# A second conditioning weight loaded in two parts, more zero matmuls at the start, and the hand-written orders redone, in a two-layer modulated block on one core

## The reference

```python
def _layer_norm(x, gamma, beta, eps=1e-05):
    mean = jnp.mean(x, axis=(-2, -1), keepdims=True)
    var = jnp.mean(jnp.square(x - mean), axis=(-2, -1), keepdims=True)
    return (x - mean) * jax.lax.rsqrt(var + eps) * gamma + beta
h = _noise_encoding(t, E)                    # 16 x 128, sines and cosines
h = jax.nn.silu(h @ W1 + b1)                 # 128 -> 512
h = h @ W2 + b2                              # 512 -> 512, the second conditioning weights
scale = (h @ Wsc + bsc)[:, None, :]          # 512 -> 256
shift = (h @ Wsh + bsh)[:, None, :]
out = jax.nn.silu(scale * _layer_norm(x, gamma, beta) + shift)
out = out @ W_in + b_in
out = jax.nn.silu(scale * _layer_norm(out, gamma, beta) + shift)
out = out @ W_out + b_out
return out + x
```

## Time and profile before

| | us |
|---|---|
| median of the 3 runs shown | 84.63 |
| the three runs | 84.8, 84.63, 81.25 |
| the profiled execution, its own time | 81.66 |
| its span, from the first to the last instruction | 79.8 |
| PE busy in the span | 74.1 (93%) |
| DVE busy | 65.0 (81%) |
| ACT busy | 55.4 (69%) |
| POOL busy | 46.1 (58%) |

### The profile page before, as it was taken

The page is one execution under the profiler, slowest core; times in us unless marked ns, Lnnn a source line. Parts: engine busy times, 40 slices in busy tenths (PEclk is TensorE's granted clock), DMA queues, the critical chain, the costliest instruction groups (busy, mean ns, idle before and its releaser), DMA issues.

```text
span 79.8 us, 1246 instructions
## 1 busy us (share of the span) xinstructions
PE 74.1 (93%) x289; PEld 39.2 (49%) x289; DVE 65.0 (81%) x211; ACT 55.4 (69%) x170; POOL 46.1 (58%) x52
## 2 busy tenths in 40 slices
PE   4979599999899999999999999999999999999950
PEld 1326474957735545445445344544444535484630
DVE  1197755599999999999998999999966499996650
ACT  4213043198795999999998799999999695785000
POOL 3000585596798999999999998968902024000000
PEclk9999985899999999999999999999999999999999
DMA  0999999999700000000240071203042003027463
GB/s 27 348 363 371 418 385 388 407 416 417 291 16 0 0 4 0 0 0 0 109 158 0 0 263 49 90 4 131 0 159 104 0 4 131 0 103 267 156 263 131
DMA packets 5047, 11.92 MB, mean 149 GB/s; under 512 B 688, under 2 KB 1200, under 8 KB 4912
## 3 DMA queue, kind: packets, MB, share of 16 engines
q1 hardware_dynamic: 4608, 11.41, 37.4%
q10 hardware_dynamic: 432, 0.45, 1.7%
HBM read 7.65 MB, written 4.19 MB: 148 GB/s over the span
## 4 chain that ended last, share of the span: by engine, by line
PE 80%; DMA 10%; DVE 3%; SPq 2%; ACT 1%; issue 1%
PE acc L935 31%; PE acc L955 31%; DMA gamma_sb<-gamma_dram 10%; PE acc L966 4%; PE acc L943 3%; PE acc L839 3%; PE acc L845 2%; DVE bn L551 1%; PE stat L916 1%; DVE o_sb L636 1%; PE acc L858 1%; SPq L267 1%; PE stat L891 1%; PE stat L885 1%; PE acc L852 1%; ACT acc L417 1%
## 5 line engine op out<-in xcount | busy, mean ns | idle before, releaser
L393 ACT ACTIVATE act<-act,cond 128x256 f32<-128x256 f32 x64 | 35.9, 593 | 5.4 <-DVE act L631 2.1
L935 PE MATMUL acc<-act,win_sb 128*128 128x512 f32 x56 | 26.5, 603 | 0.0
L955 PE MATMUL acc<-act,wout_sb 128*128 128x512 f32 x56 | 25.9, 599 | 0.0
L409 ACT ACTIVATE squares<-acc,shift 128x256 bf16<-128x256 f32 x32 | 14.7, 467 | 1.8 <-DVE shift L608 1.3
L955 PEld LDWEIGHTS acc<-act,wout_sb 128*128 128x128 f32 x56 | 10.2, 190 | 10.7 <-issue 7.6
L331 POOL TENSOR_TENSOR act<-act,beta_sb 128x512 f32<-128x512 f32 x11 | 14.2, 1298 | 1.7 <-DMA beta_sb<-beta_dram 1.1
L935 PEld LDWEIGHTS acc<-act,win_sb 128*128 128x128 f32 x56 | 10.0, 190 | 10.2 <-issue 8.4
L624 DVE SCALAR_TENSOR_TENSOR act<-acc,shift,gamma_sb 128x256 f32<-128x256 f32 x32 | 14.4, 475 | 0.2 <-ACT squares L409 0.2
L326 POOL TENSOR_TENSOR act<-act,gamma_sb 128x512 f32<-128x512 f32 x11 | 13.9, 1275 | 0.7
L636 DVE SCALAR_TENSOR_TENSOR o_sb<-acc,const_sb,x_sb 128x512 f32<-128x512 f32 (+1 forms) x18 | 11.9, 685 | 1.9 <-PE acc L955 1.3
L631 DVE SCALAR_TENSOR_TENSOR act<-act,rstd,beta_ps 128x512 f32<-128x512 f32 x16 | 11.8, 741 | 0.8 <-issue 0.8
(11 more groups left out here) (74 smaller groups left out, 62.2 us busy)
## 6 DMA issues: line engine op xcount, KB each, us to landing
x_sb<-x_dram SPq DMA_DIRECT2D x8, 512.0 KB, 12.0
out_dram<-o_sb SPq DMA_DIRECT2D x13, 256.0 KB, 2.0
w_sb<-w_dram SPq DMA_DIRECT2D x1, 1024.0 KB, 7.5
wss_sb<-wss_dram SPq DMA_DIRECT2D x1, 768.0 KB, 9.2
out_dram<-o_sb SPq DMA_DIRECT2D x3, 128.0 KB, 2.1
w_sb<-w_dram SPq DMA_DIRECT2D x1, 256.0 KB, 2.8
gamma_sb<-gamma_dram SPq DMA_DIRECT2D x1, 256.0 KB, 7.7
beta_sb<-beta_dram SPq DMA_DIRECT2D x1, 256.0 KB, 9.4
```

What stands on the lines that cost most here:

```text
L393: return nc.scalar.activation(buf[:, c, b], buf[:, c, b], ACT.Silu, bias=cond[:, c, 1, i:i + 1], scale=cond[:, c, 0, i:i + 1], **kw)
L409: nc.scalar.activation(squares[:, i % N_SQUARES], y_slot(p, c)[:, b], ACT.Square, bias=shift2[:, p, c, b:b + 1], accum_out=stat_in[:, p, B ...
L935: mm = nc.tensor.matmul(y_slot(p, c)[:].rearrange("p b s -> p (b s)"), win_sb[:, k, c * P:(c + 1) * P], act1[:, p, k].rearrange("p b s -> ...
L955: mm = nc.tensor.matmul(bank_of(("O", p, c, 0, BP))[:].rearrange("p b s -> p (b s)"), wout_sb[:, k, c * P:(c + 1) * P], act2[:, p, k].rear ...
```

## The change

There are four parts.

1. `w2` comes in two transfers: three quarters before `gamma`, the last quarter behind it. `rows_product` begins on the three quarters, and waits for the last quarter on a semaphore of its own (`w2_last_in`). On ACT the copy to `h2_rows` is put ahead of the copy of `gamma`.
2. There are four more matmuls of zeros: `warm(3)` ahead of the product with `w2`, and `warm(2)` in place of `warm(1)` ahead of `last_conditioning(0)`.
3. On DVE, `mean_b` and `b_in_c` move from the middle of pair 2's statistics to those of pair 0. `stats1_square(1)` goes ahead of `h2`, and `weigh_gamma(0, 0)` behind it. On PE `variance1(1)` goes ahead of the product with `wss`, and the product for `mean_b` ahead of `variance1(0)`. On POOL, `weigh_beta(0, 1)` goes behind `centre1(1, 1)`.
4. The orders of the pipeline on PE, ACT, DVE and POOL are rewritten: which half or sample of a pair goes first, and where the small statistics steps stand between the large ones. The same operations are run, in the same numbers.

```diff
-            sp.dma_start(w2_sb[:], w2).then_inc(w2_in, 16)
+            sp.dma_start(w2_sb[:, 0:KH - 1], w2[:, 0:KH - 1]).then_inc(w2_in, 16)
             sp.dma_start(gamma_sb[:], gamma).then_inc(gamma_in, 16)
+            sp.dma_start(w2_sb[:, KH - 1:KH], w2[:, KH - 1:KH]).then_inc(w2_last_in, 16)
             sp.dma_start(wss_sb[:, 0:KH - 1], wss[:, 0:KH - 1]).then_inc(wss_in, 16)
...
             centre1(0, 1)
             weigh_gamma(0, 1)
-            weigh_beta(0, 1)
             layer1_rstd(1)
             centre1(1, 1)
+            weigh_beta(0, 1)
...
+            act.wait_ge(h2_rows_mm, 1)
+            nc.scalar.activation(h2_rows[:], h2_rows_ps[:, 0, 0:P], ACT.Identity).then_inc(h2_rows_ready, 1)
             act.wait_ge(gamma_in, 16)
             nc.scalar.activation(gamma_ps[:], gamma_sb[:], ACT.Identity).then_inc(gamma_ps_ready, 1)
-            act.wait_ge(h2_rows_mm, 1)
-            nc.scalar.activation(h2_rows[:], h2_rows_ps[:, 0, 0:P], ACT.Identity).then_inc(h2_rows_ready, 1)
...
-            variance1(0)
             pe.wait_ge(const_in, 16)
             for c in range(C):
                 mm = nc.tensor.matmul(stat_m[:, 0:1], mean_w[:], const_col(COL_BIN, c), start=(c == 0), stop=(c == C - 1))
             mm.then_inc(mean_b_mm, 1)
+            variance1(0)
+            warm(3, acc[3])
             pe.wait_ge(h1_ready, KH)
             pe.wait_ge(w2_in, 16)
-            rows_product(h2_rows_ps, h1, lambda k, j: w2_sb[:, k, j * P:(j + 1) * P]).then_inc(h2_rows_mm, 1)
+            rows_product(h2_rows_ps, h1, lambda k, j: w2_sb[:, k, j * P:(j + 1) * P], range(KH - 1))
+            pe.wait_ge(w2_last_in, 16)
+            rows_product(h2_rows_ps, h1, lambda k, j: w2_sb[:, k, j * P:(j + 1) * P], range(KH - 1, KH)).then_inc(h2_rows_mm, 1)
             mean1(1)
             pe.wait_ge(h2_rows_ready, 1)
             transposed(h2_ps, h2_rows).then_inc(h2_mm, 1)
             warm(2, acc[3])
+            variance1(1)
             pe.wait_ge(h2_ready, 1)
             pe.wait_ge(wss_in, 16)
-            rows_product(cond_rows_ps, h2, lambda k, j: wss_sb[:, k, j], range(KH - 1)).then_inc(cond_rows_mm, 1)
-            variance1(1)
-            warm(1, acc[1])
+            rows_product(cond_rows_ps, h2, lambda k, j: wss_sb[:, k, j], range(KH - 1), KH - 2).then_inc(cond_rows_mm, 1)
+            warm(2, acc[1])
```

More of the change, by code:

```diff
@@ L359, in _ @@
             layer2_rstd(2)
+            centre1(5, 0)
             centre1(5, 1)
-            centre1(5, 0)
+            weigh_gamma(5, 0)
             weigh_gamma(5, 1)
-            weigh_gamma(5, 0)
+            weigh_beta(5, 0)
             weigh_beta(5, 1)
-            weigh_beta(5, 0)
             layer2_rstd(3)
@@ L482, in _ @@
+            square2(4, 0, 0)
+            activate2(3, 1, 1)
             activate2(3, 0, 0)
             activate2(3, 0, 1)
-            activate2(3, 1, 0)
-            activate2(3, 1, 1)
+            square2(5, 0, 1)
+            square2(5, 0, 0)
+            activate1(6, 0, 0)
+            activate1(6, 1, 0)
             square2(5, 1, 1)
+            activate1(6, 1, 1)
+            activate1(6, 0, 1)
+            activate2(4, 1, 0)
             square2(5, 1, 0)
-            activate1(6, 1, 0)
@@ L686, in _ @@
             stats1_square(2)
+            stats1_spread(2)
             dve.wait_ge(wsum_ready, 1)
             weigh_sums(0)
[L689 to L694 removed]
             add_sums(0)
@@ L775, in _ @@
-            finish(2, 0, 0, BP)
-            normalise2(3, 0)
-            weigh_sums(5)
-            normalise2(3, 1)
-            add_sums(5)
-            weigh_gamma(6, 0)
-            mean_shift2(5)
-            weigh_beta(6, 0)
-            variance2_half(4)
-            stats1_variance(7)
-            weigh_gamma(7, 0)
-            variance2(4)
+            finish(2, 1, 0, BP)
+            stats1_spread(7)
+            normalise2(3, 1)
+            weigh_sums(5)
+            weigh_gamma(6, 0)
@@ new lines, in _ @@
+            add_sums(5)
+            normalise2(3, 0)
+            weight2(4, 0, 0)
+            weight2(4, 0, 1)
+            variance2_half(4)
+            mean_shift2(5)
+            variance2(4)
+            stats1_variance(7)
+            weigh_beta(6, 0)
+            finish(2, 0, 0, BP)
+            weight2(5, 0, 1)
+            weigh_gamma(7, 0)
+            normalise2(4, 1)
+            weight2(5, 0, 0)
+            normalise2(4, 0)
+            weigh_beta(7, 0)
+            finish(3, 0, 0, BP)
@@ L839, in warm, with rows_product @@
                     nc.tensor.matmul(bank[:].rearrange("p b s -> p (b s)"), zeros[:, 0:P], zeros[:], start=True, stop=True)
-            def rows_product(rows_ps, h, w, ks=range(KH)):
+            def rows_product(rows_ps, h, w, ks=range(KH), last=KH - 1):
                 for k in ks:
@@ L845, in rows_product @@
                         mm = nc.tensor.matmul(rows_ps[j * ROWS:(j + 1) * ROWS, 0, 0:P], h[:, k], w(k, j),
-                                              start=(k == 0), stop=(k == ks[-1]), tile_position=(0, j * ROWS))
+                                              start=(k == 0), stop=(k == last), tile_position=(0, j * ROWS))
                 return mm
@@ L1016, in _ @@
             layer1_first(0, 1, 1)
+            mean2(0)
             layer1_first(1, 1, 1)
-            mean2(0)
             mean1(3)
@@ L1023, in _ @@
             layer1(1, 0, 1)
-            mean1(4)
             layer1(1, 1, 1)
             mean2(1)
+            mean1(4)
             layer1(2, 0, 0)
@@ L1029, in _ @@
             layer1(2, 0, 1)
+            mean2(2)
             layer1(2, 1, 1)
             variances(1)
-            mean2(2)
             layer2(0, 0, 0)
             layer2(0, 1, 0)
+            mean1(5)
             layer2(0, 0, 1)
-            mean1(5)
             layer2(0, 1, 1)
@@ L1040, in _ @@
             layer1(3, 1, 1)
+            layer1(3, 0, 1)
             variances(2)
             mean2(3)
-            layer1(3, 0, 1)
             layer2(1, 1, 0)
```

277 lines of the change are left out of this document (131 added, 146 removed), and 20 rows, old and new, of tables (PRODUCTS, SQUARES, WEIGHTED).

## The result

The changed kernel took a median of 82.56 us in 4 runs (82.11, 82.41, 82.72 and 84.89), beside a median of 82.94 us in 4 runs of the kernel before (84.8, 84.63, 81.25 and 80.92). The runs that were disturbed, as by a low clock, are left out of the ratios. The ratio of after to before is 1.0177, with a 95% interval of 1.0098 to 1.0255: 0.0177 x 80.9 us, the shortest run of before, or about 1.4 us slower. The whole interval lies above 1, so a loss is shown; whether it is over 2% is not. The forecast was 80.9 us, a gain. The profiled execution is the one of 84.89 us, with a span of 83.1. It is the slowest of the four, because its whole start ran at half speed; the other times are not told from it.

What follows compares the result with a forecast made beforehand. A transfer, `gamma`, bounded the kernel up to 10.3 us, and PE almost without a break from 16.98 us. An earlier pair 1 gains 0.8 us, the orders 0: 81.66 - 0.8 = 80.9 us, range 80.1 to 84.2.

Steps and rivals of the forecast that it cites:

- part 4: Pipeline orders: same number of operations and no idle PE time to remove, so a change of 0 us.
- far bound: Pipeline hand-overs: at most 0.6 us lost, from PE's nearest measured waits of 0.23 us, two or three times.
- the orders open gaps: Rival, pipeline: PE waits for DVE's small steps, together 0.6 us or more; 81.5 us, up to 82; chance 0.15.
- A gain of 0.85 us: Start: pair 1's products begin at 21.1 us instead of 21.96, where both strands meet; taken as 0.8 us.
- first yardstick: Chances of faster or slower: executions like the profiled one and the 81.25 us run, weight 0.6.
- part 3: DVE's statistics of pair 2: start at 16.25 us instead of 16.72, 0.25 us shorter; pair 3's `part` at 20.9 us.
- conditioning strand: Start: `wss` product 0.81 us instead of 1.44, its last quarter's landing decides, first `layer1` product at 16.2 instead of 16.98 us.
- reading of the long runs: Two runs of before, 3.4 us above the shortest: clock low for about two stretches more, 1.7 us each.
- a later fall: Rival: clock falls under pair 0's products; 82.6 us for one stretch, 84.3 for two; chance 0.17.
- the clock as before: Rival, start: zeros ahead of `w2` don't hold the clock, pair 1 begins only about 0.35 us earlier; 81.3 us; chance 0.15.
- the small transfer's latency: Rival, DMA queue: the quarter of `w2` holds it for 2 us, delaying `x` of pair 2; 82.8 us; chance 0.03.
- I am wrong if PE shows over 0.3 us of waits in the pipeline: Sign against the forecast, in the pipeline: PE waits there totalling more than 0.3 us.

Runs made afterwards that it cites:

- a1: The changed kernel, unaltered, run again: median 81.91 us, ratio to before 1.0145.
- a4: The kernel before with the new pipeline orders alone: median 82.32 us, ratio 1.0107 (0.9965 to 1.025).
- a2: The kernel before with `w2` in two transfers, four more zero matmuls and the statistics moved, old pipeline orders: median 81.1 us, ratio 1.0042.
- a3: The kernel before with the four more zero matmuls alone: median 81.13 us, ratio 1.0053.
- c4: The kernel before with only three more zero matmuls, ahead of the product with `w2`: median 81.19 us, ratio 1.0094.
- b1: The kernel before, unaltered, run again: median 84.83 us.
- b3: The changed kernel with `add_sums(5)` moved ahead of `weigh_gamma(6, 0)` on DVE: median 82.02 us, ratio 1.0227.
- c2: The kernel before with `weigh_gamma(6, 0)` and `add_sums(5)` moved ahead of `normalise2(3, 1)` on DVE: median 83.15 us, no ratio.
- d3: The kernel before with two zero matmuls ahead of the product with `w2`: median 80.98 us, ratio 1.004.

## Why the prediction was wrong

**The step that failed: part 4, "Over all such hand-overs I take 0 and keep 0.6 us as the far bound".** It measured 0.97 to 0.99 us in the three profiles with the new orders unaltered (after, a1, a4). The reason given, that the orders "change no number of operations, and PE has no idle time there to take away", holds for instructions of fixed duration. One of them is not fixed: DVE's gamma step went from 0.98 to 1.72 us because its new place is beside POOL's gamma step. I looked for hand-overs between DVE and PE that came earlier, and named `mean2(2)`; up to 19.4 us behind the start of pair 1, past that place, the new orders lose nothing. I did not look at what runs on POOL while a moved DVE step runs. The far bound was taken from waits of PE, which are effects; the two durations of that very step in the trace of before, 0.74 and 0.98 us, were the rows that say it is not fixed. An estimate from them: there it ended 0.56 us after POOL's step, so beside the start of a POOL step of 1.27 us it takes up to 1.27 + 0.56 = 1.8 us, 1.1 more than alone. The rival "the orders open gaps" was right in kind, with 81.5 us and up to 82, and it was given 0.15.

By the Trainium skill, page "SBUF — State Buffer", section "SBUF: two separate sides", DVE and GpSimd share a port pair that is taken as a lock for a whole instruction, and a DVE operation with two SBUF inputs is blocked by a GpSimd operation that reads SBUF. The trace agrees: 1.72 us beside POOL's step, against 0.74 for the form with gamma in PSUM, and 0.74 for L631 with beta in PSUM beside the same step. The lock is not quite total by these rows, since the step ends 0.55 us after POOL's, less than its 0.74.

**The second step: the sum was made against an execution that had a loss in it.** "A gain of 0.85 us" is the difference from the 21.96 us of the earlier trace rows, behind the low clock of the earlier trace rows. By the landing rule above, the same execution with a held clock would have begun pair 1 at 13.9 + 7.5 = 21.4 us on the chain instead of 22.10, with the old start. So nearly all of the 0.8 us of the forecast is what removing the fall is worth. It shows in medians (81.1 and 81.13 us in a2 and a3 beside 81.84 for before on the same chip, 81.19 in c4 beside 82.84), and not against undisturbed executions, where the start alone is at 1.0042. The prediction used the profiled execution as its first yardstick, though it had itself priced the fall in it. With both terms put right the loss against undisturbed runs comes out: 0.99 us for the orders and 0.0042 x 80.9 = 0.3 us for the start are 1.3 us, against 1.4 measured (1.2 by the ratio of a1).

**A third step, hidden by luck: part 3.** It counted 0.25 us for the two instructions that leave pair 2's statistics, and `x` of pair 2 as what is late next. Neither is so. In a2, DVE's statistics of pair 2 start at 15.94 us, not 16.25, with no wait for `x`; pair 3's `part` ends 4.88 us later, exactly as long as before, since the variance between waits for PE at 19.25 us. From the first `layer1` product to pair 1 it is 5.12 us, as before. An earlier start and a strand that was not shortened cancel, and pair 1 came where it was forecast.

**What held.** In a2 the times of the start came nearly as forecast: the last quarter of `w2` at 10.61 us (10.3 forecast), the clock at 1.00, the product with `wss` at 0.79 us (0.81), the first `layer1` product at 16.20 (16.2), and pair 1 at 21.18 by the timeline that the earlier trace rows comes from (21.1; 21.32 on the chain). The conditioning strand was right in its mechanism too: the fall goes, and the landing of `wss` decides. That the split is worth nothing at the end was right: zeros alone (a3, 1.0053) and zeros with the split (a2, 1.0042) can't be told apart. By the record three zeros hold the clock in 63 of 64 executions, near enough as taken. The reading of the long runs as further stretches of low clock is borne out by b1. The rivals of a later fall, of the clock as before and of the small transfer's latency occurred in no profile with the extra zeros; the one execution of a2 at 0.959 is not profiled.

**Against the conditions named.** "I am wrong if PE shows over 0.3 us of waits in the pipeline" was meant for this loss and would have missed it: the busy counts of the kernel after show 0.24 us of idle time in the pipeline, and 0.99 us are lost. The length of the pipeline is the sign to name. The clock record of the changed kernel's profiles never fell below 1.00 after 15 us. The half-speed start of both profiles of the changed kernel, and of b3, was not foreseen at all. It raised pair 1 to 24.3 us in 84.8 us executions, and in b3, where it lasted until about 23.5 us, to 28.22 us in one of 88.66 us. It may not be special to the change: three executions of the kernel before took 84.04 to 84.06 us with a recorded clock of 0.999, and c2, with the old start, has two at 84.87 and 84.98 us with 1.00. None of these has a profile, and what brings such a start about was not tried.

## What to carry to other kernels

When a hand-written order is redone, check for every moved instruction what runs beside it on the other engines, not only who waits for it: the range of durations that one form shows in the trace says which steps have a price. If a form has 0.74 us in one place and 0.98 in another, its neighbour is part of its cost, and the cheapest fix may be to move it by two places. Before a gain is worked out against a profiled execution, take the disturbances out of that execution: a fix for an occasional fall of the clock lowers the median and leaves the best executions where they were. From the runs here I would keep the old orders with two zeros ahead of `w2` (median 80.98 us), which cannot be told from the kernel before in undisturbed runs (1.004, 0.9988 to 1.0092).

## What the runs showed of the hardware beyond that

- The lengthening works both ways. POOL's beta step took 1.27 us alone (the kernel before at 12.95 us) and 1.53 to 1.54 us where DVE's gamma step was still running when it began (b3 at 56.84, c2 at 50.96).
- POOL's centring step (`centre1`, L322) holds the gamma step too: in the kernel after it ends at 57.28 us, and the second gamma step, begun at 56.87, takes 0.95 us and ends 0.54 us after it.
- The clock record can read 1.00 while PE runs at half speed: in the kernel after, zeros of 0.43 us each until about 14 us under a recorded 1.00. A time per instruction of one form, 56 against 33 ns, is the safer sign.
- Landings of one transfer in one place of the queue differ by over 1 us between executions (13.49 to 14.66 us for the last quarter of `wss`), more than the whole effect that was studied.
- Without the extra zeros seven of eight profiles show a low clock soon after PE's idle time ahead of `w2` (a4 alone does not); with them none of ten does (after, a1 and b3 among them, whose start was at half speed all along). But a4 (0.92 us idle) and d3 (0.99 us idle, with two zeros) held it, and 35 of 76 timed executions of before show no fall, so the idle time makes it possible, not certain.
